# A two-layer graph network kernel: the first edge stage with paired 64-row gate matmuls, a bf16 one-hot and the edge weight moved onto the one-hot

## The reference

```python
dk = silu(edge_attr @ Wdk.T + bdk)      # edge_attr: 64 features per edge
dv = silu(edge_attr @ Wdv.T + bdv)
attn = sum(q[dst] * k[src] * dk, axis=1)
attn = silu(attn) * cosine_cutoff(edge_weight)
msg = v[src] * dv * attn[:, None]
agg = segment_sum(msg, dst)
```

## Time and profile before

| what | value |
|---|---|
| median of 3 runs | 4749.34 us (4734.86 to 4750.56) |
| span of the profiled execution, first to last instruction | 4737.6 us |
| PE busy | 4031.9 us (85%) |
| DVE busy | 4120.2 us (87%) |
| POOL busy | 3352.1 us (71%) |
| ACT busy | 2900.4 us (61%) |

### The profile page before, as it was taken

The page is one execution under the profiler, slowest core; times in us unless marked ns, Lnnn a source line. Parts: engine busy times, 40 slices in busy tenths (PEclk is TensorE's granted clock), DMA queues, the critical chain, the costliest instruction groups (busy, mean ns, idle before and its releaser), DMA issues. The chain is left out here.

```text
span 4737.6 us, 112614 instructions
## 1 busy us (share of the span) xinstructions
PE 4031.9 (85%) x23408; PEld 3334.4 (70%) x23408; DVE 4120.2 (87%) x13250; ACT 2900.4 (61%) x8405; POOL 3352.1 (71%) x3818
## 2 busy tenths in 40 slices
PE   0778888888888878999799898999999898968887
PEld 0357777777777767899677777777777677757776
DVE  6779999999999995555599999999999999968887
ACT  0765555555555543333488888888888888862222
POOL 0568888888888861111488888888888888857776
PEclk9989999999999998999888888888888888879899
DMA  2568777777777775666577777777777777776664
GB/s 75 179 206 250 229 228 228 228 228 227 228 229 228 228 190 174 202 200 197 168 207 206 204 206 204 206 204 205 205 204 206 204 204 204 205 158 189 176 170 133
DMA packets 647755, 950.12 MB, mean 201 GB/s; under 512 B 215768, under 2 KB 490760, under 8 KB 647287
## 3 DMA queue, kind: packets, MB, share of 16 engines
q0 software_dynamic: 153600, 510.70, 38.4%
q1 hardware_dynamic: 494043, 438.22, 32.1%
HBM read 777.56 MB, written 171.03 MB: 200 GB/s over the span
## 5 line engine op out<-in xcount | busy, mean ns | idle before, releaser
L1385 POOL DMA_INDIRECT kv1c<-kv_table,rec x936 | 916.8, 980 | 305.5 <-issue 175.2
L741 POOL DMA_INDIRECT kv<-kv_table,rec x864 | 921.3, 1066 | 247.3 <-issue 241.8
L1439 ACT ACTIVATE wv<-kv1c,wv 128x64 f32<-128x64 f32 x3744 | 927.7, 334 | 2.1
L1517 DVE CUSTOM_DVE_ANT_0 masked_scores<-score_p,mask 126x384 f32<-126x384 f32 x1248 | 679.5, 545 | 11.4 <-issue 5.8
L1615 PE MATMUL sum_p<-wv,hot 128*126 128x260 f32 x1872 | 626.3, 482 | 2.3 <-ACT wv L1439 2.3
L908 PE MATMUL sum_p<-msg,hot 128*126 128x256 f32 x1728 | 433.6, 394 | 192.2 <-DVE msg L864 192.2
L1577 PE MATMUL qe_p<-qrel,hotT 126*128 126x256 f32 x1872 | 546.9, 436 | 21.0 <-ACT hotT L1417 14.2
L1374 POOL TENSOR_SCALAR hot<-iota,local 128x126 f32<-128x126 f32 x936 | 549.7, 600 | 0.3 <-issue 0.2
L908 PEld LDWEIGHTS sum_p<-msg,hot 128*126 128x126 f32 x1728 | 309.4, 189 | 280.5 <-DVE msg L864 213.2
L1577 PEld LDWEIGHTS qe_p<-qrel,hotT 126*128 126x128 f32 x1872 | 428.8, 229 | 108.2 <-ACT hotT L1417 14.4
L1615 PEld LDWEIGHTS sum_p<-wv,hot 128*126 128x126 f32 x1872 | 398.4, 228 | 89.8 <-ACT wv L1439 2.7
(11 more groups left out here) (222 smaller groups left out, 10254.0 us busy)
## 6 DMA issues: line engine op xcount, KB each, us to landing
key<-segment_keys SPq DMA_DIRECT2D x312, 189.0 KB
q_blk<-q_table SPq DMA_DIRECT2D x216, 192.5 KB
acc_table<-acc SPq DMA_DIRECT2D x312, 128.0 KB
qrel<-q_by_relation SPq DMA_DIRECT2D x312, 126.0 KB
acc_in<-acc_table SPq DMA_DIRECT2D x50, 767.8 KB
q_by_relation<-qrel SPq DMA_DIRECT2D x50, 756.0 KB
feat<-in_edge_feat_t SPq DMA_DIRECT2D x216, 128.0 KB
agg_table<-total SPq DMA_DIRECT2D x216, 126.0 KB
```

The lines of the kernel that those rows point to most:

```text
L741: pool.indirect_dma_start(kv[k][:, t, :], None, c["kv0_d"], bass.IndirectOffsetOnAxis(ap=rec[k][:, t, 0:1].bitcast(I32), axis=0)).then_inc ...
L1385: pool.indirect_dma_start(kv[k][:, t, :], None, c["kv1_d"], bass.IndirectOffsetOnAxis(ap=rec[k][:, t, 0:1].bitcast(I32), axis=0)).then_inc ...
L1439: ins = act.activation(wv[k][:, t, h, 0:DK], kv[s][:, t, D + h * DK:D + (h + 1) * DK], ACT.Copy, scale=wv[k][:, t, h, DK:DK + 1])
L1517: dve.tensor_tensor_reduce(junk[k][:, h, :], score_p[:, h, :], mask[it.slot(4)][:], 1.0, -BIG, ALU.add, ALU.max, top[s][:, h:h + 1]).then_ ...
```

## The change

Four things are done in `edges_0`, and the features are laid out otherwise on the host.

- **Gates.** Features come as 128 partitions x 2 x 128: partitions 0 to 63 hold the 64 features of tiles 0 and 1, partitions 64 to 127 those of tiles 2 and 3, so the weights of every matmul are contiguous. A tile has now four matmuls of 64 contraction rows: bias, leading x leading weights, leading x rest of the weights, rest x leading weights. The two tiles of a pair lie on different halves of the rows and in different PSUM banks, and their matmuls alternate. One ACT copy of 256 columns replaces two of 512; POOL's subtraction is 128x256 in place of 64x512. POOL does it between the second and the third gather.
- **One-hot.** Made by one DVE instruction straight from the records, in bf16; the small `local` instruction is gone. Its transpose on PE is bf16.
- **Weight.** `messages` no longer multiplies with the edge's weight: it is one tensor_tensor of 1024 columns. ACT multiplies the one-hot with the weight (`weigh_hot`, four activations of 126 columns), and `sum_messages` takes the weighted one-hot.
- **Order.** ACT: `hot_out`(s-1), `split_lead`(s), first half of `gates_silu`(s-1), `attn_silu`(s-2), second half of `gates_silu`(s-1), `weigh_hot`(s-2). DVE: `q_times_k`(s-2), `one_hot`(s), `scores`(s-2), `same_block`(s), `messages`(s-2), `weights`(s-2), `add_total`(s-3). PE's order stays.

```diff
-                    sp.dma_start(feat[k][:], c["edge_feat_t"][:, ds(edge, CH0)]).then_inc(loaded[k], 16)
+                    sp.dma_start(feat[k][:], c["edge_feat_t"][:, :, ds(col, P)]).then_inc(loaded[k], 16)
...
-                    pool.tensor_tensor(parts[k][R:P, :], feat[s][:], parts[k][0:R, :],
-                                       ALU.subtract).then_inc(parts_ready, 1)
-
-                run_chunks(pool, steps, ((1, split_rest), (0, gather)))
+                    pool.tensor_tensor(rest[k][:], feat[s][:], lead[k][:], ALU.subtract).then_inc(rest_ready, 1)
+
+                run_chunks(pool, steps, ((0, gather((0, 1))), (1, split_rest), (0, gather((2, 3)))))
...
-                    act.copy(parts[k][0:R, :], feat[s][:]).then_inc(lead_ready, 1)
-                    act.copy(lead[k][0:R, :], feat[s][:]).then_inc(lead_ready, 1)
+                    act.copy(lead[k][:], feat[s][:]).then_inc(lead_ready, 1)
...
-                def gates_silu(it):
-                    k = it.slot(2)
-                    wait(act, msg_ready, it, 2)
+                def gates_silu(half):
+                    def f(it):
+                        k = it.slot(2)
+                        if half == 0:
+                            wait(act, msg_ready, it, 2)
+                        for at in (2 * half, 2 * half + 1):
+                            t = TILE_ORDER[at]
+                            act.wait_ge(gates_summed, it.count(1, T0, at + 1))
+                            act.activation(gates[k][:, t, :], gates_p[t][:], ACT.Silu).then_inc(gates_ready, 1)
+                    return f
+
+                def weigh_hot(it):
+                    k = it.slot(2)
+                    wait(act, weight_ready, it)
+                    wait(act, msg_summed, it, 2)
                     for t in range(T0):
-                        act.wait_ge(gates_summed, it.count(1, T0, t + 1))
-                        act.activation(gates[k][:, t, :], gates_p[t][:], ACT.Silu).then_inc(gates_ready, 1)
-
-                run_chunks(act, steps, ((1, hot_out), (0, split_lead), (2, attn_silu), (1, gates_silu)))
+                        ins = act.activation(hot_w[k][:, t, :], hot[it.slot(4)][:, t, :], ACT.Copy,
+                                             scale=weight[k][:, t:t + 1])
+                    ins.then_inc(hot_w_ready, 1)
+
+                run_chunks(act, steps, ((1, hot_out), (0, split_lead), (1, gates_silu(0)), (2, attn_silu),
+                                        (1, gates_silu(1)), (2, weigh_hot)))
...
+                    dve.scalar_tensor_tensor(hot[it.slot(4)][:],
+                                             c["iota"][:].rearrange("p (o n) -> p o n", o=1).to_broadcast([P, T0, GROUP]),
+                                             first_of(s), rec[s][:, :, 1:2].to_broadcast([P, T0, GROUP]),
+                                             ALU.add, ALU.is_equal).then_inc(hot_ready, 1)
...
-                    for t in range(T0):
-                        ins = dve.scalar_tensor_tensor(msg[k][:, t, :], kv[s][:, t, D:2 * D], weight[k][:, t:t + 1],
-                                                       gates[k][:, t, D:2 * D], ALU.mult, ALU.mult)
-                    ins.then_inc(msg_ready, 1)
-
-                run_chunks(dve, steps, ((2, q_times_k), (0, locate), (2, scores), (0, one_hot), (2, weights),
-                                        (3, add_total), (2, messages)))
+                    dve.tensor_tensor(msg[k][:], kv[s][:, :, D:2 * D], gates[k][:, :, D:2 * D],
+                                      ALU.mult).then_inc(msg_ready, 1)
+
+                run_chunks(dve, steps, ((2, q_times_k), (0, one_hot), (2, scores), (0, same_block), (2, messages),
+                                        (2, weights), (3, add_total)))
...
-                        pe.matmul(gates_p[t][:], parts[k][:, t::T0], w_lead[:], start=True, stop=False)
-                        pe.matmul(gates_p[t][:], lead[k][:, t::T0], w_rest[:], start=False,
-                                  stop=True).then_inc(gates_summed, 1)
+                        tiles = [(TILE_ORDER[2 * pair + h], slice(h * R, (h + 1) * R)) for h in range(2)]
+                        for t, rows in tiles:
+                            pe.matmul(gates_p[t][:], ones_r[rows, :], b_rows[rows, :], start=True, stop=False)
+                        for t, rows in tiles:
+                            pe.matmul(gates_p[t][:], lead[k][rows, pair, :], w_lead[rows, :], start=False, stop=False)
+                        for t, rows in tiles:
+                            pe.matmul(gates_p[t][:], lead[k][rows, pair, :], w_rest[rows, :], start=False, stop=False)
+                        for t, rows in tiles:
+                            pe.matmul(gates_p[t][:], rest[k][rows, pair, :], w_lead[rows, :],
+                                      start=False, stop=True).then_inc(gates_summed, 1)
...
                 def sum_messages(it):
                     k = it.slot(2)
+                    wait(pe, hot_w_ready, it)
                     wait(pe, msg_ready, it)
                     wait(pe, total_ready, it, 1)
                     for t in range(T0):
-                        ins = pe.matmul(sum_p[:, k, :], hot[it.slot(4)][:, t, :], msg[k][:, t, :],
+                        ins = pe.matmul(sum_p[:, k, :], hot_w[k][:, t, :], msg[k][:, t, :],
```

More of the change, by code:

```diff
@@ L637, in edges_0 @@
         kv = [sb(f"kv{k}", [P, T0, 2 * D]) for k in range(U)]
-        local = [sb(f"local{k}", [P, T0]) for k in range(2)]
-        hot = [sb(f"hot{k}", [P, T0, GROUP]) for k in range(4)]
+        hot = [sb(f"hot{k}", [P, T0, GROUP], BF16) for k in range(4)]
+        hot_w = [sb(f"hot_weighted{k}", [P, T0, GROUP]) for k in range(2)]
         hotT = [sb(f"hotT{k}", [GROUP, T0, P], BF16) for k in range(2)]
@@ L795, in _ @@
                 dve.wait_ge(filled, U + 2)
[L796 to L804, removed]
@@ L808, in _, with one_hot @@
+                dve.tensor_copy(b_lead[:], b_raw[:]).then_inc(w_lead_ready, 1)
+                dve.wait_ge(w_lead_ready, 2)
+                dve.tensor_tensor(w_rest[:], w_raw[:], w_lead[:], ALU.subtract).then_inc(w_ready, 1)
+                for h in range(2):
+                    row = slice(h * R + BIAS_REST, h * R + BIAS_REST + 1)
+                    dve.tensor_tensor(b_rows[row, :], b_raw[row, :], b_lead[row, :], ALU.subtract).then_inc(w_ready, 1)
                 steps = chunk_steps(dve, c["steps0"])
-                def locate(it):
-                    k, s = it.slot(2), it.slot(U)
+                def one_hot(it):
+                    s = it.slot(U)
@@ L812, in locate @@
                     wait_slot(dve, loaded, it, LOADS)
-                    wait(dve, total_ready, it, U)
-                    last = s if isinstance(it.i, int) and it.index == 0 else it.prev().slot(U)
-                    dve.tensor_scalar(keep[s][:], first_of(s)[0:GROUP], first_of(last)[0:GROUP], None, ALU.is_equal)
-                    wait(dve, hot_ready, it, 2)
-                    dve.tensor_scalar(local[k][:], rec[s][:, :, 1], first_of(s), None,
-                                      ALU.subtract).then_inc(local_ready, 1)
@@ L821, in one_hot @@
[L821 to L827 removed]
+                    wait(dve, hot_w_ready, it, 4)
@@ L847, in add_total @@
                     k, s = it.slot(2), it.slot(U)
+                    wait(dve, keep_ready, it)
                     wait(dve, msg_summed, it)
@@ L856, in weights @@
                     wait(dve, attn_act_ready, it)
+                    wait(dve, hot_w_ready, it, 2)
                     dve.tensor_tensor(weight[k][:], attn_act[k][:], rec[s][:, :, 3], ALU.mult).then_inc(weight_ready, 1)
```

112 lines of the change are left out of this document (62 added, 50 removed).

## The result

The changed kernel took **5276.7 us** (median of 4 runs, 5265.9 to 5282.5) beside 4745.1 us for the kernel before (median of 4): a ratio of 1.112, 95% interval 1.110 to 1.114. The forecast was 5216 us. The profiled execution took 5282.5 us, with a span of 5280.6.

The account below looks back on a forecast made before the run. The prediction took POOL to bound the kernel at 6.65 us per chunk in edges_0. A new period of 8.81 us gave 216 x (8.81 - 6.65) = +467 us on the 4749.3 us median, 5216 us, range 4985 to 5390.

Parts of the forecast that it names:

- The step that decides: In edges_0, ACT's new order with PE's old one makes PE's sum wait for the weighted one-hot: 7.89 us per chunk.
- the ring: In edges_0, PE sum, q, first gates, ACT silus, weighing, PE sum again: closed once per step, 7.89 us.
- Clock: In edges_0, new idle lowers PE's granted clock to 0.87, taking the period from 7.89 to 8.81 us.
- the two bounds: edges_0 period at the lower clock: 8.55 us if slow time falls on PE's part in proportion, 9.07 if all does.
- Edges_0 as a whole: The stage's total change: 216 x (8.81 - 6.65) = +467 us.
- The upper bound of the ring: In edges_0, the period with ACT's weighing at its high bound of 2.1 us: 8.76 us.
- Gates in pairs: In edges_0, PE runs a pair's two matmuls together: eight rounds at 0.23 us, with 0.25 us of overlap with q lost.
- POOL's subtraction: In edges_0, POOL's subtraction goes from 512 to 256 columns, from 1.27 to about 0.64 us.
- "faster" rival: In edges_0, POOL stays the bound and gets lighter: 5.99 us per chunk, -143 us, 4607 us; chance 0.05.
- The other stages are not touched: Outside edges_0 nothing changes: the cost is 216 times the period, other stages add zero.
- Full clock: In edges_0, the ring forms but PE keeps its full clock: +268 us, 5017 us; chance 0.25.
- Blocked POOL: In edges_0, DVE's 1024-column message product keeps POOL out 1.13 us: 6.74 us per chunk, +19, 4768 us; chance 0.03.

Follow-up runs that it names:

- e2: Changed kernel with ACT weighing before the gate silus and DVE making weights before messages, plus DVE fillers: 4728.7 us, 0.996 of the kernel before.
- e4: Changed kernel with ten unused bf16 matmuls per chunk in PE's idle time, plus DVE fillers: 5011.4 us, 1.057 of the kernel before.
- e6: Changed kernel with all four gate matmuls of one tile ahead of the other tile's, plus DVE fillers: 5359.2 us, 1.098 of the kernel before.
- e11: The kernel of e2 unchanged, run once more beside e9: 4735.7 us, 0.997 of the kernel before.
- e9: The kernel of e2 with each chunk's message product cut into four one-tile multiplications: 4650.1 us, 0.979 of the kernel before.

## Why the prediction was right

- **"The step that decides."** Right: the ring closes in every chunk, and e2 takes it away by order alone. Its length at full clock was put at 7.89 us and is 7.82; ACT 2.03 against 2.02, weighing 1.26 against 1.28, PE 4.40 against 4.44.
- **Clock.** 0.87 was taken from edges_1, 0.88 measured; 8.81 us per chunk against 8.74. The term was worth 199 us in the sum, and e4 measured 201. The choice between the two bounds, slow time falling on PE's part and falling on all, was an average of two ideas and was lucky to that degree. The long turns show where it falls: all on PE's sum and q, which start behind the idle (1.25 + 0.47 us), and nothing on the gates or on ACT. It is more than the 0.66 us of the lower bound because the mean clock of 0.88 also counts time in which PE runs at the full one.
- **Edges_0 as a whole:** +467 forecast, +461 measured, and both terms by themselves: 268 for the length against 259, 199 for the clock against 201. The upper bound of the ring was added up wrongly (8.76; its terms give 2.03 + 2.1 + 4.40 + 0.20 = 8.73), and nothing hung on it.
- **Gates in pairs.** Eight rounds of 0.23 us, as taken, but for the first, which took 0.34; e6 shows the halves side by side in either order. From the start of q to the start of the gates it is 1.41 us where it was 1.23, so 0.18 of the 0.25 us of overlap that the forecast took as lost are lost. By the rule of the Trainium skill (TensorEngine Tiling (Array Packing), Key Properties) a switch of mode drains the engine. The trace agrees with it in kind; the rule has no size.
- **POOL's subtraction** was mis-sized: 0.64 us forecast by its columns. It is 0.72 to 0.74 us when nothing disturbs it and a median of 0.90 in the changed kernel. Half the columns took away 0.54 of 1.28 us, so some 0.2 us of it doesn't go with the columns, by estimate from these two. It cost nothing on the ring, but it and the stretched gather are why e2 doesn't reach the 5.99 us of the forecast's "faster" rival.
- **"The other stages are not touched"** is the step that missed: it put them at nothing. The span grew by 543 us where the sum had 467. The 76 us between are the 96 of edges_1, less 16 of nodes_out and 6 by which edges_0 came out shorter, and a small rest. Shorter code ahead of a loop is a change to that loop's place. The cause of the 16 stays open.
- **The rivals.** Full clock (5017): e4 gives that case, 5011, when PE is kept busy. Blocked POOL: its mechanism is real in e2, where one gather takes 1.61 us (1.84 in e11, 0.66 and 0.89 longer than the others, against the 1.13 that this rival had); without the ring it gave 4729, under this rival's 4768. By the Trainium skill (SBUF — State Buffer, Who interferes with whom) a DVE instruction with two SBUF inputs contends with a GpSimd instruction that reads SBUF. e9 agrees: cut in four, the product with two SBUF inputs leaves the gather at 0.95 us, and so does the long product that has one input in PSUM.

## What to carry to other kernels

Before moving work to a less busy engine, write down for each step which item every engine works on and close the loops by hand: a step that one engine puts last and another wants first makes a ring in every step, and with in-order queues its length is the period, whatever the busy shares say. Ask the same of each part of a change by itself; here one part gains 2.6% and the other loses 5.2%. And look at stages that were not touched: a loop can get slower because the code ahead of it got shorter.

## What the hardware showed unexpectedly

- By where it lies, DVE's loop in edges_1 has instructions fetched anew in every turn or hardly any (three places tried, two of them lose): 182 packets against 6 in the stretch, a stop of 4.1 us (144.6/35) per turn. 92 fillers remove it, 36 put it into the kernel before.
- Matmuls on disjoint halves of the rows can overtake each other: with four of one tile ahead of four of the other in the program, the records still pair at one start per 0.23 us (e6).
- The length of a single DVE instruction with two SBUF inputs, and not only the sum of such work, bears on what POOL's transfer issue costs: 1.61 or 1.84 us beside one product of 1024 columns (e2, e11), 0.95 beside four of 256 (e9) and beside a product of 1024 columns with one input in PSUM.
- PE's granted clock falls with short idle stretches, if they come in every chunk: 2.1 us ahead of the sum in a turn of 7.8 gave 0.88 and cost 201 us; with 1.05 us of idle and ten dummy matmuls it stayed at 1.00 (e4).
